# One GNN kernel: buffers split ten and ten between rows by source and by destination, and three more weight chunks loaded early

## The reference, cut to what matters

```python
h = relu(layernorm(x))
# first layer: each edge has a kind: edges 0..127 hh, 128..767 oo, the rest ho
feat = concat([h[src], h[dst]], axis=1)              # 8448 x 2048
e = relu(feat @ W_kind + b_kind)                      # W_kind 2048 x 1024
logit = e @ W_a + b_a
alpha = softmax of logit over the edges of each destination
z = segment_sum(alpha * h[src], dst)                  # 256 x 1024
o = relu(concat([h, z]) @ W_hn + b_hn) for rows 0..63, with W_on, b_on for the others
x = x + o
# second layer: W is 1024 x 1024, zero but for the sums of edge weights at (src, dst)
x = x + relu(layernorm(x)) @ W.T + bias
```

## Time and profile before

| | us |
|---|---|
| median of 3 runs | 329.81 (329.73 to 329.83) |
| span of the profiled execution | 328.4 |

### The profile page before, as it was taken

The page is one execution under the profiler, slowest core; times in us unless marked ns, Lnnn a source line. Parts: engine busy times, 40 slices in busy tenths (PEclk is TensorE's granted clock), DMA queues, the critical chain, the costliest instruction groups (busy, mean ns, idle before and its releaser), DMA issues.

```text
span 328.4 us, 4177 instructions
## 1 busy us (share of the span) xinstructions
PE 309.0 (94%) x1376; PEld 197.6 (60%) x1381; DVE 253.7 (77%) x434; ACT 176.3 (54%) x437; POOL 161.6 (49%) x148
## 2 busy tenths in 40 slices
PE   0899999999999999999999999969998999999995
PEld 0687688845667666466575756646644554456543
DVE  4655446547999988999679898689988998998354
ACT  3854433182467654658656458545338396393202
POOL 3030057405877788787857888558788430000000
PEclk9999999999999999999999999987999899999999
DMA  7999979999999999999999999999999999999604
GB/s 255 402 399 407 368 247 316 399 402 334 366 357 413 409 410 409 409 408 410 419 408 411 408 409 409 416 412 408 410 408 411 410 406 409 402 409 410 246 0 128
DMA packets 34425, 122.06 MB, mean 372 GB/s; under 512 B 4058, under 2 KB 4570, under 8 KB 34404
## 3 DMA queue, kind: packets, MB, share of 16 engines
q0 software_dynamic: 19008, 69.21, 54.0%
q1 hardware_dynamic: 14004, 47.34, 37.3%
q10 hardware_dynamic: 1392, 5.24, 3.9%
HBM read 115.49 MB, written 6.29 MB: 371 GB/s over the span
## 4 chain that ended last, share of the span: by engine, by line
DMA 32%; PE 25%; POOL 22%; DVE 9%; issue 7%; ACT 3%; ACTq 0%; DVEq 0%
DMA Gq<-q_ho,ids 31%; PE psG L852 13%; POOL Gp L369 12%; POOL Gq L383 10%; PE psG L963 5%; DVE Gp L668 3%; PE psG L1071 2%; PE psG L1066 1%; DVE Gp L672 1%; DMA xs<-x 1%; PE psW L902 1%; ACT h L404 1%; DVE Wl L621 1%; ACT Wh L413 1%; DVE st L597 1%
## 5 line engine op out<-in xcount | busy, mean ns | idle before, releaser
L668 DVE TENSOR_TENSOR Gp<-Gp,Gq 128x1024 f32<-128x1024 f32 x65 | 79.3, 1221 | 24.3 <-DMA Gq<-q_ho,ids 21.6
L369 POOL DMA_INDIRECT Gp<-p_ho,ids x60 | 75.6, 1259 | 44.2 <-DMA p_ho<-T 24.3
L383 POOL DMA_INDIRECT Gq<-q_ho,ids x60 | 69.0, 1149 | 39.8 <-issue 14.9
L994 PE MATMUL psG<-W,hT 128*128 128x512 f32 x192 | 85.6, 596 | 0.0
L672 DVE SCALAR_TENSOR_TENSOR Gp<-Gp,wa 128x1024 f32<-128x1024 f32 x65 | 79.1, 1217 | 0.4
L478 ACT ACTIVATE RW<-ohs,ewh 128x256 fp32r<-128x256 f32 x66 | 33.2, 503 | 51.4 <-DVE ohs L659 47.1
L994 PEld LDWEIGHTS psG<-W,hT 128*128 128x128 f32 x192 | 35.7, 192 | 39.5 <-issue 39.0
L902 PE MATMUL psW<-RW,ohd 128*128 128x256 f32 x264 | 44.9, 293 | 0.1
L902 PEld LDWEIGHTS psW<-RW,ohd 128*128 128x128 f32 x264 | 36.7, 191 | 3.3 <-issue 2.9
L902 PE MATMUL psA<-RL,ohd 128*128 128x256 f32 x240 | 36.3, 296 | 2.2 <-ACT RL L488 1.6
L621 DVE TENSOR_TENSOR Wl<-W,Wh 128x1024 fp32r<-128x1024 f32 x16 | 19.6, 1223 | 22.2 <-ACT Wh L413 22.2
(11 more groups left out here) (177 smaller groups left out, 357.7 us busy)
## 6 DMA issues: line engine op xcount, KB each, us to landing
W<-weights SPq DMA_DIRECT2D x63, 512.0 KB, 7.4
Gp<-weights SPq DMA_DIRECT2D x8, 512.0 KB, 10.1
Gq<-weights SPq DMA_DIRECT2D x4, 512.0 KB, 10.1
pre_f<-weights SPq DMA_DIRECT2D x3, 512.0 KB, 7.4
xs<-x SPq DMA_DIRECT2D x2, 512.0 KB, 3.8
h_rows<-h ACTq DMA_DIRECT2D x1, 1024.0 KB, 6.8
pre_l<-weights SPq DMA_DIRECT2D x2, 512.0 KB, 7.2
p_ho<-T ACTq DMA_DIRECT2D x2, 512.0 KB, 4.7
```

The source lines that it names most:

```text
L369: nc.gpsimd.indirect_dma_start(out=Gp[:, i % NP, :], out_offset=None, in_=p_oo if t <= OO_TILES else p_ho, in_offset=bass.IndirectOffsetOn ...
L383: nc.gpsimd.indirect_dma_start(out=Gq[:, i % NQ, :], out_offset=None, in_=q_oo if t <= OO_TILES else q_ho, in_offset=bass.IndirectOffsetOn ...
L668: nc.vector.tensor_tensor(Gp[:, i % NP, :], Gp[:, i % NP, :], Gq[:, i % NQ, :], ALU.add).then_inc(s_sum, 1)
L994: last = nc.tensor.matmul(psG[:, 2 * t + half, :], hT[:, k, t * P:(t + 1) * P], W[:, s, half * HALF:(half + 1) * HALF], start=u != 1 and k ...
```

## The change

The number of places in `Gp` falls from 12 to 10, that in `Gq` rises from 8 to 10. `PRE` rises from 9 to 12: one chunk more goes past the ring while the split chunks run (`PRE_HEAD` 6, in a third place under `RL`), and six instead of four go into places 4 to 9 of `Gq`. The loads of these six are no longer laid one by one between the loads of ring chunks 16 to 20; they stand behind chunk 20, and the ring loads wait for their own places alone. GpSimd issues p_rows(0..9), q_rows(0..9), and then q_rows(i), p_rows(i) in turn; q_rows(4..9) wait for the use of W_hh chunks 6 to 11 (before, q_rows(4..7) waited for chunks 5 to 8). At the end the first chunk of W_hn takes the place of `Gp` ahead of `rows_h`, and the order of SyncE's loads stays as it was; `rows_h` now waits for the logit of tile 61, the first four chunks of W_hn for those of tiles 59, 62, 63 and 64. The second layer's bias goes into the ring `W` instead of `Gp`.

```diff
-NP = 12
-NQ = 8
+NP = 10
+NQ = 10
...
-PRE_HEAD = 5
-PRE = PRE_HEAD + 4
+PRE_HEAD = 6
+PRE = PRE_HEAD + 6
 TOPS = SPLIT + HH - PRE + PLAIN
...
-ROWS_AT = FREED + len(LAST_SLOT)
+HN_IN_GP = 4
+HN_FIRST = FREED + len(LAST_SLOT)
+ROWS_AT = HN_FIRST + 1
 ROW_SLOT = ROWS_AT % NP
-HN_AT = ROWS_AT + NT
-HN_IN_GP = 4
-HN_SLOT = [(HN_AT + k) % NP for k in range(HN_IN_GP)]
-BREP_AT = HN_AT + HN_IN_GP
-BREP_SLOT = BREP_AT % NP
+HN_AT = [HN_FIRST] + [ROWS_AT + NT + k for k in range(HN_IN_GP - 1)]
+HN_SLOT = [at % NP for at in HN_AT]
+BREP_Q = TOPS + 2 * LAST_TOP + KC - HN_IN_GP
...
-        _, pre_l = shared(("rl_low", [P, D], f32), ("pre_l", [P, 2, D], f32))
+        pre_l, = shared(("pre_l", [P, 3, D], f32))
...
-        brep = Gp[:, BREP_SLOT, :]
+        brep = W[:, BREP_Q % WSLOTS, :]
...
+            def load_pre(n):
+                sp.dma_start(pre[n], weights[(SPLIT + n) * P:(SPLIT + n + 1) * P, :]).then_inc(s_pre[n], 16)
+
...
-                if HALVES < q < SPLIT and q % 2 and q // 2 - 2 < PRE_HEAD or SPLIT <= q < SPLIT + PRE - PRE_HEAD:
-                    n = q // 2 - 2 if q < SPLIT else PRE_HEAD + q - SPLIT
-                    if q >= SPLIT:
-                        sp.wait_ge(s_wused, q - HALVES + 1)
-                    sp.dma_start(pre[n], weights[(SPLIT + n) * P:(SPLIT + n + 1) * P, :]).then_inc(s_pre[n], 16)
+                if HALVES < q < SPLIT and q % 2 and q // 2 - 2 < PRE_HEAD:
+                    load_pre(q // 2 - 2)
+                elif q == SPLIT + HALVES:
+                    for n in range(PRE_HEAD, PRE):
+                        sp.wait_ge(s_wused, min(SPLIT + n - PRE_HEAD - HALVES + 1, SPLIT))
+                        load_pre(n)
...
-                    sp.wait_ge(s_used, HN_AT + k + 1)
+                    sp.wait_ge(s_used, HN_AT[k] + 1)
...
-            sp.wait_ge(s_used, BREP_AT + 1)
+            sp.wait_ge(s_wused, uses_before(BREP_Q))
             sp.dma_start(brep, l1_bias.broadcast_to((P, D))).then_inc(s_lb, 16)
```

More of the change, by code:

```diff
@@ L86 @@
 LATE_TILES, LAST_TILES, HN_TILES = 56, 61, 62
-assert BREP_AT < len(GATHERED)
+assert HN_AT[-1] < len(GATHERED)
+assert KC - HN_IN_GP < WSLOTS
 assert FREED_Q % NQ + 3 <= NQ
@@ L193, in gnn_block @@
         den = sb("den", [P, NT], f32)
-        pre = [pre_f[:, n, :] for n in (1, 2, 0)] + [pre_l[:, n, :] for n in range(2)]
+        pre = [pre_f[:, n, :] for n in (1, 2, 0)] + [pre_l[:, n, :] for n in range(3)]
         pre += [Gq[:, HALVES + n, :] for n in range(PRE - PRE_HEAD)]
```

## The result

| | before | after |
|---|---|---|
| median, us | 329.82 | 336.88 |
| runs, us | 329.73 to 331.30 | 335.77 to 337.51 |
| span of the profiled execution, us | 328.4 | 335.7 |

One execution of after took 350.86 us; it counts in the median of four, but, like executions of the experiments that stand as far above the others of their kernel, neither in the range nor in the ratio.

The account below looks back on a forecast made before the run. The prediction took the volume moved by the DMA engines to bound the long middle, the last gather setting the end. Terms 1.8 + 3.6 - 2.0 = 3.4 us gave 333.2 us, with a range from 328.0 to 337.0 us.

Parts of the forecast that it names:

- deficit of the pause, by 102 us: GpSimd's q_rows wait for W_hh chunks from 85 to 94.5 us; net 1.4 units less moved, 1.8 us lost.
- overtaking: At the end, SyncE's last loads, released by tile 60, get in ahead of the last gathers: 2.8 units, 3.6 us.
- VectorE's catch-up: At the last tiles, VectorE finishes 2.5 us after the last landing instead of 4.5: 2.0 us gained.
- tail behind the last logit: Chain of small steps from the last logit to the end, taken as unchanged at 33.2 us.
- the gain of one: Up to the gathers of q_rows(6), three early chunks more and two gathers of p fewer: one unit more moved.
- from there on the engines are saturated: After the pause, DMA runs saturated with the same total volume, so the deficit can't be won back.
- The signs named in advance: Trace marks expected: early GB/s, GpSimd waits, dip, ring loads, 410 GB/s, tile 60, last gather, VectorE waits, 33 us tail.
- The faster one, with the gap covered: Rival: the pause starves nobody or last loads stay behind; last landing before 292.7 us, likeliest 328 us; chance 0.20.
- The slower one, by the last loads: Rival: x or the last W_hn chunks bound the new rows, up to 3 us more, 336.2 us; chance 0.18.

Follow-up runs that it names:

- last_late: The changed kernel with load_last and rows_h waiting for the sum of tile 63 instead of tiles 60 and 61: 334.95 us, ratio 1.017.
- eleven_nine: The kernel before with eleven places for p and nine for q, its early chunks kept: 332.93 us, ratio 1.011.
- lead_four: The changed kernel with p_rows(i+4) ahead of q_rows(i) on GpSimd from i = 6: 329.18 us, ratio 1.0016.
- split_again: Second run of ten and ten places with the nine early chunks and load order of the kernel before: 335.60 us, ratio 1.018.
- after_again: The changed kernel once more, no edit, for its spread and a second profile: 338.26 us, ratio 1.027.
- four_early: The changed kernel with ten early chunks instead of twelve, four instead of six in Gq, GpSimd's order unchanged: 336.18 us, ratio 1.023.
- ring_ahead_again: Second run of the kernel before with the loads of ring chunks 17 to 20 ahead of the four early chunks in Gq: 328.98 us, ratio 0.9992.
- rows_ahead: The changed kernel with p_rows(i+3) ahead of q_rows(i) on GpSimd from i = 7: 330.64 us, ratio 1.0017.
- four_rows_ahead: The changed kernel with p_rows(i+3) ahead of q_rows(i) from i = 7 and ten early chunks, four in Gq: 331.73 us, ratio 1.008.
- last_soon: The kernel before with the four loads of load_last waiting for the sum of tile 57 instead of 60: 331.10 us, ratio 1.0046.

## Why the prediction was right in sign and wrong in size

Its sum was 1.8 + 3.6 - 2.0 = 3.4 us. The two profiled spans differ by 7.3 us. What the terms measured:

| term | taken, us | measured, us | from |
|---|---|---|---|
| deficit of the pause, by 102 us | 1.8 | 3.3 | 69.3 - 66.7 = 2.6 units |
| rate below 410 GB/s after 102 us | 0 | 1.4 | 31 x 6 / 524.3 + 3 x 138 / 524.3 = 1.1 units |
| overtaking | 3.6 | 3.2 | 219.3 - 216.8 = 2.5 units |
| VectorE's catch-up | -2.0 | -1.9 | 4.5 us before, 2.6 after |
| tail behind the last logit | 0 | 1.3 | 34.5 - 33.2 us |

The sum is 7.3 us. The overtaking is the volume moved by the last landing: 391 GB/s x 290.7 us before and 385 GB/s x 298.6 us after, in units. SyncE's queue alone gives the same, (40.29 - 38.94) / 0.5243 = 2.6 units. The first three terms are bookkeeping of one volume, so it is no test of them that they add up to the last landing; `last_late`, `eleven_nine` and `lead_four` are. The last gather's 7.9 us are the first three terms. The second comes from 102 to 108 us (380 GB/s, before 411) and from 147 to 285 us (407, before 410).

**The failed step** is the deficit. The prediction put it as "by 102 us seven units have landed since q_rows(6)", against "four to five", and took 1.1 to 1.8 units off after the gain of one. The landings came nearly so: the issues of 88.95, 90.67, 94.49 and 95.80 us, each with 5.7 us behind it, would give four landings between 94.7 and 101.5 us. But landings are not volume. Before, at 102 us a queue of gathers up to 10 us old (the one issued at 91.97 us landed at 104.3) was out and in part moved; after, the oldest gather still out was that of 97.05 us. By volume the pause costs 4.4 units from 84 to 102 us, not 2.1 to 2.8; that the difference lies in the part-moved ones is worked out, not seen (the landings after take the 5.7 us of the earlier trace rows, which was before's). The gain from 44 to 76 us was under-counted too, 2.7 units for one, and 0.9 units more went in stretches that the prediction did not look at. So the net is 2.6 (3.2 in the second profile of after) for 1.4. And "from there on the engines are saturated" was too early. With GpSimd alone issuing, a gather goes every 1.42 us (0.94 or 1.29 us and 0.30 us of issue), which is 0.524 MB / 1.42 us = 369 GB/s, and there are no loads from SyncE before 97.39 us plus their landing. The rate of after is 284 GB/s from 96 to 102 us and 380 from 102 to 108 us; it is at 410 GB/s only from about 108 us. The range's upper bound for this term, 1.8 units, was therefore too low, and with it 337.0 us barely holds the result of 336.88.

**Overtaking** was right in size (2.5 units for 2.8), and that was luck. Tile 60 was not summed "some 2.2 us sooner" but at 283.60 us, 1.3 us later than before (282.26 in the earlier trace rows). For that case the prediction had "1.0 unit". Why it was later is not shown: the deficit works that way, but in this profile the sums of tiles waited for no gather from 100 to 284 us, so VectorE's own work, behind TensorE's slow stretch, set the moment; in the second profile, without that stretch, it was 282.72 us. What was missed is the same as above: the loads move bytes for some 7 us before one counts as landed, and share from their issue on, not from their first landing. For the same reason the 1.3 units taken for before were 2.9. The last gather lands 298.6 - 284.8 = 13.8 us after the first of these loads was issued, before it was 290.7 - 283.5 = 7.2 us; with every other unit SyncE's, that is 5.4 and 2.8 units, 2.6 more, and the queues' bytes say 5.5 and 2.9. `eleven_nine` and `split_again` show it without a pause, and `lead_four` shows that it is no larger than before's when the last tiles lack one gather only. By the Trainium skill (DMA: Bandwidth & Descriptors, Queues, rings and completion order) each DMA engine serves its queues in turn, packet by packet; the trace of after agrees with it from 285 to 293 us, with 1.65 MB for SyncE's queue and 1.62 MB for that of the gathers.

**VectorE's catch-up** was right. In after the last logit is done 2.6 us behind the last landing, before 4.5 us.

**The tail** was taken as unchanged, "33.2 us". It is 34.5. TensorE's two profiles, before and after:

```profile
295.36 1.99 PE L902 MATMUL psA<-RL,ohd 128*128 128x256 f32 x12
297.19 1.88 PE L1016 MATMUL psG<-Gp,hT 128*128 128x512 f32 x4
```

```profile
302.64 0.72 PE L907 MATMUL psA<-RL,ohd 128*128 128x256 f32 x4 [2.12 <-ACT RL L493]
303.21 3.18 PE L1021 MATMUL psG<-Gp,hT 128*128 128x512 f32 x4
```

And after's stretch from 304 to 306 us:

```profile
304.00:306.00 2.00, 2.00 (x3) 0.34 (x1) 1.93 (x6) 0.60 (x2) 0.00 (x0) 0.50 1.02 410
```

Where the last tile waits for DMA, TensorE waits with it, 2.12 us ahead of the last counts. Then its granted clock from 304 to 306 us is 0.50, the 1.2 GHz level, and the same four matmuls take 3.18 us instead of 1.88: 1.3 us on the chain. In the five profiles in which VectorE waited more than 2 us for a gather at one of the last two tiles (after, `after_again`, `split_again`, `four_early`, `eleven_nine`) this group took 2.95 to 3.62 us and the tail 34.4 to 35.1 us. In the six in which it didn't (before, `ring_ahead_again`, `rows_ahead`, `lead_four`, `four_rows_ahead`, `last_soon`) the group took 1.88 us and the tail 33.1 to 33.2 us. A wait on one engine had a price on the next one's clock, and the sum had no term for it.

**The signs named in advance.** Right: more GB/s from 44 to 56 us (352), GpSimd waiting for L963's products (3.08, 0.78 and 1.81 us), the dip near 90 us, ring loads from 97.6 us (97.39), VectorE waiting for gathers at the last tiles (at 63 and 64; 61 and 62 came without a wait). Wrong: 410 GB/s to the end (407 from 147 to 285 us), tile 60 sooner (it was later), the last gather at 295 to 297 us (298.6), 33 us behind the last logit (34.5, over the 34 that was named as a sign of error).

**The rivals.** The faster one, with the gap covered, fell at its own test: the last landing came at 298.6 us, not before 292.7. The slower one, by the last loads, did not come about by its mechanism, though the time would have fitted (336.2 us): VectorE waited 2.6 us for x in the tail against 4.8 us before, and what made the tail longer was TensorE's clock.

**What stays open.** The traces add up, the times less well: by the ratios pause and split together cost 6.8 and 8.9 us, the split alone 4.7 and 6.1, and a shorter pause (`four_early`) 7.5. That the pause costs time of its own therefore rests on the traces. About 2 us of the split's median (`split_again`) stand in no trace, since its profiled execution was its fastest. And the 1.4 us of rate after 102 us were 0.7 us at most in the second profile of after (410 GB/s from 147 to 285 us), with a deficit by 102 us that was 0.6 units larger; the border between the two terms is not sharp. None of the kernels was measurably faster than before.

## What to carry to other kernels

In a queue that runs in order, an instruction that must wait goes behind all those whose buffers are free: the same twelve early chunks and the same ten and ten places cost 7 to 9 us with q_rows ahead and nothing measurable with p_rows four ahead. Where volume bounds the kernel, a pause is to be counted in bytes moved, from the first issue that is missing until the rate is back at its full value, and not in landings. And whatever an earlier completion releases onto another DMA queue shared the engines with the last gathers one for one here, so the question for each released load is how many of the last needed transfers are still to move at that moment.

## What the runs showed of the hardware

- GpSimd's gathers of 512 KB issued back to back leave one per 1.42 us, by which they would move 369 GB/s alone, an estimate, against the 410 measured with SyncE's loads beside them.
- TensorE can fall into a slow stretch in the middle of its work (39.15 us busy of 51 at a granted clock of 0.83, from 96 to 147 us) which in another execution of the same kernel isn't there (50.25 us at 1.00). It cost no time here: the last gather landed at 298.6 and 298.8 us.
- With both queues full, SyncE's loads and GpSimd's gathers got the same share of the DMA engines (1.65 and 1.62 MB in 8 us). When few of the gathers' bytes were left, their last 0.20 MB took the same 5.1 us as 1.84 MB of SyncE's.
- On TensorE 2.1 us of idle time were followed by a granted clock of 0.50 and a group of matmuls that took 3.18 us instead of 1.88.
- The volume moved by 102 us differed by 1.9 units (69.3 and 71.2) between two kernels with the same code up to there.
